# A three-layer decoder on one core: the last steps of its first stage in a hand-written order per engine

## The chip, the cores and the metric

The kernel runs on one core of a Trainium2 chip. The metric is the time of one execution in device microseconds (us). The core has five engines with an instruction queue each, taken in order: TensorE (PE in the rows; its weight loads are PEld), VectorE (DVE), ScalarE (ACT), GpSimd (POOL) and SyncE (SP), which here only starts transfers. The engines meet by semaphores, and products land in eight PSUM banks of 128 x 512 float32 words.

## The reference, cut to what matters

The input is x, 16 batches of 128 tokens with 256 features. It passes three layers, each followed by a layernorm of (input + layer).

```python
# layer 1, for each batch b
h        = layernorm(x) * g + b
lin_out  = linear_attention(h @ wq_lin, h @ wk_lin, h @ wv_lin)     # one division per token
win_out  = window_attention(h @ wq_loc, h @ wk_loc, h @ wv_loc)     # 16 heads
gate     = sigmoid(relu(concat(lin_out, win_out, h) @ wg1 + bg1) @ wg2 + bg2)
layer    = (gate * lin_out + (1 - gate) * win_out) @ wo + bo + x
x        = layernorm(x + layer)
# layer 2: cross-attention of x with a context, 16 heads
# layer 3: 32 experts, each token goes to 4 of them, plus a shared expert
```

To keep float32 accuracy most products are made of float16 halves: a value is cast to a "high" part, the difference to it is the "low" part, and a product is high x high + high x low + low x high.

## The kernel before, in words

There are three stages, one after the other: layer 1 (lines 180 to 1220), layer 2 with the routing (from line 1300 on), and the experts. Between the first and the second stands a barrier of all engines (lines 1233 to 1235, with the clearing of the semaphores between).

**The first stage as a pipeline.** One loop per engine runs over steps i; each step calls small functions for batches that lag behind i. A batch n is at normalisation in step n, at its scores in step n+3, has its attention weights transposed (`transposed`, L978) and applied (`weighted`, L990) in steps n+4 and n+5, has both branches transposed (`branches_T`, L1060) in step n+5 together with the first gate product (`gate1`, L1076), the second gate product (`gate2`, L1089) in step n+6, the output product (`out_proj`, L1100 and L1104) in step n+7, and its residual sum and statistics on VectorE (`yt_` L855, `st2` L862 and L865) in step n+8, followed on GpSimd by the reciprocal root (`pow2`, "vareps" and "rstd") and the normalisation (`x1`, L472). So batch 15, the last one, goes on until step 23, while there are fewer and fewer other batches to work on: this is the drain.

**What stands between the products of one batch.** `lwf` (L587) takes the transposed branches out of PSUM, `lwhi` (L593) casts them, `lwlo` (GpSimd, L428) takes the low part: then `gate1` may run. `z1f_` (L600), `z1hi` (L607) and `z1lo` (GpSimd, L451): then `gate2`. `gt_` (L616), then on GpSimd `ma`, `mb`, `mhi`, `mlo` (L398, L406, L480, L436), which blend the two branches: then `out_proj`. `ls` and `ld` (L414, L421) make sum and difference of the branches beforehand on GpSimd.

**What orders the work.** The order of the calls in each engine's loop, and the table `ORDERS`: it lists which products share a bank and in which turn. `Turns.wait` makes each wait until the one before it in the list has been read:

```python
["KV0", "WO", "Z2", "Z1"],      # one bank: out_proj, gate2 and gate1 take turns
```

**What the drain does besides.** In steps 20 to 22 the start of layer 2 for batch 0 (and parts for 1 and 2) is put between: on ScalarE eight casts of constants (L668 to L675), the casts of normalised input and context (`x1_high` L622, `c_high` L626); on VectorE their low parts (`x1_low` L869, `c_low` L873), `xq_low` (L877), `xk_low` (L883), the four minima (`x_mins`, L888) and their halves (L895, L897); on TensorE `x1_T` (L1115), `q_proj`, `k_proj`, `v_proj` (all L1124), the scores (L1163) and the transposed scores (L1185, L1188); on ScalarE `x1T_`, `xq_high`, `xk_high`, `xv_`, `minT_` and the exponentials `x_exps` (L657). `v_proj` for batches 0 and 1 is done here. The low halves of the second stage's weights come in 8 pieces, one per step on GpSimd (`low_part`, L367), the last two in steps 19 and 20.

**The second stage's start.** Its own loops (from L1415 on) skip what the drain has done: `FRONT = 2` batches of the projections, one of the scores. In step 4 TensorE does, in this order, the transposition of the minima (L1922), parts of the weighted sums (L1954), and the transposed scores (L1936).

## Time and profile before

| | us |
|---|---|
| median of 3 runs | 695.78 (695.25 to 698.1) |
| the profiled execution, its own time | 693.8 |
| its span, first to last instruction | 692.0 |
| the drain: from the first step with no new batch's scores left to the barrier | about 232 to 271 of the span |

In the rows of this document PE, PEld, DVE, ACT and POOL are the engines as named above. A row of the timeline has the start in us from the span's start, the duration in us, engine, line, operation, output<-inputs, how many instructions are merged in it, and in brackets how long the engine sat idle before it and what released it. Durations of instructions on one engine overlap by some hundredths of a us, so the distance between two starts is what an instruction costs in a row of them. A row of stretches has the length, then for each engine the busy time with the count of instructions, the granted TensorE clock as a share of 2.4 GHz, the share of time in which the DMA engines were busy, and GB/s.

### The profile page before, as it was taken

The numbers are of one execution on the slowest core, as the hardware profiler recorded it, in microseconds if no ns is written. First come the engines' busy times: TensorE is split into PE (matmuls) and PEld (weight loads), VectorE is DVE, ScalarE is ACT, GpSimd is POOL, SyncE is SP. The second block draws the span as 40 slices with busy tenths as digits, with TensorE's granted clock in tenths as the row PEclk, the third lists the DMA queues.
The fourth block names the chain that finished last, engine by engine and source line by source line (L and its number), as shares of the span: only waits on it lengthen the run. The fifth ranks groups of instructions, "written<-read, shape, count | busy, mean of one in ns | idle before, by whom it ended". The sixth has DMA issues, their size and how long they took to land.

```text
span 692.0 us, 24587 instructions
## 1 busy us (share of the span) xinstructions
PE 579.0 (84%) x8258; PEld 482.5 (70%) x8258; DVE 516.0 (75%) x2068; ACT 481.9 (70%) x1325; POOL 474.5 (69%) x621
## 2 busy tenths in 40 slices
PE   1899999999999966988888887766668999999393
PEld 1678889888888755766656566545658988888272
DVE  2898989898888645589999998755756776767273
ACT  3799999999899944777777777655146776676022
POOL 4667899999988975243768676453706776777583
PEclk9999999999999998999999999976999999999697
DMA  9420000000200001324465645323678566672493
GB/s 302 118 57 3 2 3 4 2 3 16 56 2 3 3 17 32 85 80 146 133 199 158 194 140 186 110 88 114 205 202 234 162 181 191 174 204 83 147 331 129
DMA packets 53642, 77.81 MB, mean 112 GB/s; under 512 B 8457, under 2 KB 42513, under 8 KB 52881
## 3 DMA queue, kind: packets, MB, share of 16 engines
q1 hardware_dynamic: 42768, 56.50, 27.8%
q0 software_dynamic: 7632, 16.87, 6.8%
q10 hardware_dynamic: 3120, 2.88, 1.2%
q8 instruction: 69, 1.13, 0.7%
q14 instruction: 53, 0.43, 0.2%
HBM read 48.62 MB, written 27.49 MB: 110 GB/s over the span
## 4 chain that ended last, share of the span: by engine, by line
PE 25%; DVE 19%; issue 8%; POOL 3%; ACT 3%; DMA 1%; DVEq 0%; ACTq 0%; POOLq 0%; SPq 0%
PE bank L2379 6%; PE bank L2408 4%; DVE mnx L1639 4%; PE bank L2397 3%; PE bank L2348 3%; PE bank L1864 2%; DVE we_lo L1679 2%; PE bank L2017 1%; DVE min_hl L1646 1%; PE bank L2389 1%; POOL ya L2198 1%; DVE min_hl L1648 1%; PE bank L1913 1%; DVE aT L1672 1%; ACT aT L1565 1%
## 5 line engine op out<-in xcount | busy, mean ns | idle before, releaser
L2190 POOL DMA_INDIRECT y_rows<-front,ix x95 | 93.8, 987 | 50.7 <-DVE ix L2294 24.8
L572 ACT ACTIVATE sc<-sc,mn 128x128 f32<-128x128 f32 x256 | 82.6, 417 | 2.2 <-DVE mn L811 2.2
L1488 POOL DMA_INDIRECT x_rows<-rows,slot_ix x64 | 65.1, 1017 | 16.3 <-issue 13.8
L2215 ACT ACTIVATE sc<-bank 128x512 f16<-128x512 f16 x95 | 56.3, 595 | 26.5 <-DVE eh_lo L2298 21.9
L811 DVE CUSTOM_DVE_ANT_0 sc<-bank,rel 128x128 f32<-128x128 f32 x256 | 57.6, 286 | 0.8 <-issue 0.5
L820 DVE TENSOR_TENSOR pT_lo<-bank,pT_hi 128x512 f16<-128x512 f32 x64 | 43.1, 675 | 5.2 <-ACT pT_hi L579 5.1
L2290 DVE COPY front<-bank 128x256 f32<-128x256 f32 x63 | 26.7, 424 | 22.9 <-PE bank L2408 22.5
L1019 PE MATMUL bank<-hT,w_hi 128*128 128x128 f16 x384 | 42.7, 225 | 1.2 <-POOL hT L382 1.0
L579 ACT ACTIVATE pT_hi<-bank 128x512 f16<-128x512 f32 x64 | 38.5, 604 | 4.4 <-PE bank L978 4.2
L978 PE MATMUL bank<-ident,sc 128*128 128x128 f32 x256 | 39.4, 276 | 1.1 <-DVE k_lo L801 1.1
L2379 PE MATMUL bank<-we_hi,sc 128*128 x252 | 37.8, 273 | 1.6 <-ACT sc L2215 1.3
L1639 DVE TENSOR_REDUCE mnx<-bank 128x4 f32<-128x512 f32 x60 | 37.2, 682 | 2.4 <-PE bank L1913 2.3
L2397 PE MATMUL bank<-ident,hT 128*128 128x128 f16 x380 | 36.6, 219 | 2.3 <-DMA hT<-x_rows 1.8
L1458 POOL TENSOR_TENSOR we_lo<-east,we_hi 128x256 f16<-128x256 f32 x48 | 31.2, 683 | 7.0 <-ACT we_hi L1521 6.8
L1466 POOL TENSOR_SCALAR xvar<-xmv 128x1 f32<-128x1 f32 x16 | 3.6, 226 | 46.5 <-DVE xmv L1703 46.5
L2237 ACT ACTIVATE sc<-bank,fshift,frstd 128x256 f32<-128x256 f32 x16 | 9.0, 564 | 34.8 <-DVE fshift L2337 25.5
L1864 PE MATMUL bank<-w_hi,front 128*128 128x256 f16 x120 | 23.7, 294 | 11.2 <-DVE front L1805 11.2
L1553 ACT ACTIVATE sc<-bank 128x512 f32<-128x512 f32 x60 | 30.9, 602 | 2.9 <-PE bank L1939 2.5
L1521 ACT ACTIVATE we_hi<-east 128x256 f16<-128x256 f32 (+1 forms) x80 | 31.2, 454 | 1.8 <-DMA east<-in_experts 1.7
L1002 PE MATMUL bank<-w_hi,hT 128*128 128x256 f16 (+1 forms) x128 | 31.8, 331 | 0.3 <-DVE vlin L763 0.3
L1019 PEld LDWEIGHTS bank<-hT,w_hi 128*128 128x128 f16 x384 | 29.4, 101 | 2.3 <-DVE w_lo L726 1.3
L2397 PEld LDWEIGHTS bank<-ident,hT 128*128 128x128 f16 x380 | 27.7, 98 | 3.3 <-issue 2.5
(333 smaller groups left out, 2338.5 us busy)
## 6 DMA issues: line engine op xcount, KB each, us to landing
east<-in_experts SPq DMA_DIRECT2D x32, 384.0 KB, 3.3
hT<-x_rows SPq DMA_DIRECT2D x95, 129.0 KB
rows<-xhl SPq DMA_DIRECT2D x16, 512.0 KB, 4.5
hT<-y_rows SPq DMA_DIRECT2D x16, 512.0 KB, 5.4
x_rows<-pad_block SPq DMA_DIRECT2D x32, 129.0 KB, 2.8
wst<-in_wcat SPq DMA_DIRECT2D x8, 256.0 KB, 6.5
front<-in_ctx_t SPq DMA_DIRECT2D x16, 128.0 KB, 3.0
out<-sc ACTq DMA_DIRECT2D x16, 128.0 KB, 4.9
```

Of the source, the lines that this page charges most:

```text
L572: done = act.activation(sc[:, g, j], sc[:, g, j], ACT.Exp, bias=mn[:, n % 2, g, j:j + 1], scale=-1.0)
L579: act.activation(pT_hi[:, g % 2], pT_bank[g][:].rearrange("p (h k) -> p h k", h=GH), ACT.Copy).then_inc(pThi_r[g], 1)
L811: dve.tensor_tensor_reduce(out=sc[:, g, j], in0=sc_bank[g][:, j * P:(j + 1) * P], in1=rel[:, g, j], scale=-1.0, scalar=-NEG, op0=ALU.add, ...
L820: dve.tensor_tensor(pT_lo[:, g % 2], pT_bank[g][:].rearrange("p (h k) -> p h k", h=GH), pT_hi[:, g % 2], ALU.subtract).then_inc(pT_rd[g], 1)
L978: last = pe.transpose(pT_bank[g][:, j * P:(j + 1) * P], sc[:, g, j], ident[:])
L1019: last = pe.matmul(room[u][:, m * P:(m + 1) * P], w[:, k, col + m * P:col + (m + 1) * P], hT[:, n, hp, k], start=t == 0 and not bias, stop ...
L1488: pool.indirect_dma_start(shared.x_rows, bass.IndirectOffsetOnAxis(ap=slot_ix[:, n, k:k + 1], axis=0), rows4[:, q, k], None).then_inc(shar ...
L1639: dve.tensor_reduce(mnx[:, n % 2, g], sc_bank[g][:].rearrange("p (h k) -> p h k", h=GH), AX_X, ALU.min).then_inc(xmn_r[g], 1)
L2190: pool.indirect_dma_start(c.y_rows, bass.IndirectOffsetOnAxis(ap=ix[:, n % IX], axis=0), yo[:, n % YO], None, bounds_check=NDEST - 1, oob_ ...
L2215: act.activation(gT[:, n % U], GT_BANK[n % len(GT_BANK)], ACT.Copy).then_inc(gt_r, 1)
L2379: done = pe.matmul(GU_BANK[n % len(GU_BANK)][:, 0:2 * EI].rearrange("p (m w) -> p m w", m=2), gT[:, n % U, x_, k], E[y_][k][:, :, bass.ds( ...
L2397: done = pe.transpose(GT_BANK[n % len(GT_BANK)][:, part, k], xg.bitcast(F16)[:, n % G, (part * KT + k) * P:(part * KT + k + 1) * P], c.ide ...
```

## The change

- Every engine's loop of the first stage now ends before the drain (TensorE after step 18, the others after step 19), and what is left is written out as a list of calls per engine, in an order of its own. On TensorE `gate1(14)` is split in two halves with `weighted(15, ...)` between.
- Six late products no longer take turns in the shared bank: `out_proj(13)` goes to bank 1, `gate2(14)` to bank 0, `out_proj(14)` to bank 5; `gate1(15)`, `gate2(15)` and `out_proj(15)` stay in bank 4 with waits of their own.
- The eight casts of constants, `x1_high` and `c_high` for batches 0 and 1, the low parts of the last two weight pieces, and batch 15's `lwlo`, `z1lo`, blend (`mixture`), and the normalisation of batches 14 and 15 (`normal`) are on VectorE in place of ScalarE and GpSimd.
- `v_proj(1)` and its `xv_(1)` move to step 4 of the second stage. `v_proj(0)` uses bank 7. `q_proj`, `k_proj` and `v_proj` wait for 4 of the 8 weight pieces, not for all.

The diff, cut to its core (12 columns of indentation are taken away):

```diff
-FRONT, FRONT_X, FRONT_C, FRONT_S = 2, 3, 3, 1
+FRONT, FRONT_X, FRONT_C, FRONT_S, FRONT_V = 2, 3, 3, 1, 1
+FRONT_PIECES = -(-(2 * D + D) // 228)
...
-POOL_PIECES = {3: (6,), 4: (7, 8), 5: (9, 10), **{k: (k - 2,) for k in range(13, 21)}}
+POOL_PIECES = {3: (6,), 4: (7, 8), 5: (9, 10), **{k: (k - 2,) for k in range(13, 19)}}
+LATE_PIECES = (17, 18)
...
+first_values = banks[7]
...
+drain_room = {("WO", NB - 3): (banks[1], (pv_rd, NB)),
+              ("Z2", NB - 2): (banks[0], (emptied["S3"], NB)),
+              ("Z1", NB - 1): (banks[4], (emptied["Z1"], 2 * (NB - 1))),
+              ("WO", NB - 2): (banks[5], (front_emptied["XT"], 2)),
+              ("Z2", NB - 1): (banks[4], (emptied["Z1"], 2 * NB)),
+              ("WO", NB - 1): (banks[4], (emptied["Z2"], 2 * NB))}
+
+def room_of(u, n):
+    return drain_room[u, n][0] if (u, n) in drain_room else room[u]
...
-        for i in range(NB + 8):
+        for i in range(NB + 4):
...
+        lwlo(NB - 2)
+        ma(NB - 3)
+        mb(NB - 3)
+        mhi(NB - 3)
+        mlo(NB - 3)
+        ls(NB - 2)
+        pow2(NB - 4)
+        z1lo(NB - 2)
+        x1(NB - 4)
+        ls(NB - 1)
+        ld(NB - 1)
+        pow2(NB - 3)
+        ma(NB - 2)
+        mb(NB - 2)
+        mhi(NB - 2)
+        mlo(NB - 2)
+        x1(NB - 3)
+        pow2(NB - 2)
+        pow2(NB - 1)
...
-        for i in range(NB + 7):
-            if i == NB + 4:
-                act.activation(ident16[:], ident[:], ACT.Copy).then_inc(id16_r, 1)
-                act.activation(identb[:], ident[:], ACT.Copy).then_inc(idb_r, 1)
-                act.wait_ge(rc_in, 64)
-                act.activation(tri16[:], tri[:], ACT.Copy).then_inc(idb_r, 1)
-                act.wait_ge(front_set, 4)
-                act.activation(ones16[:], ones[:], ACT.Copy).then_inc(idb_r, 1)
-                for k in range(GH):
-                    act.activation(pick_min[:, k], ones[:], ACT.Copy, scale=par[:, 2 + k:3 + k]).then_inc(idb_r, 1)
-                for n in range(FRONT):
-                    x1_high(n)
-                    c_high(n)
+        for i in range(NB + 4):
             z1f_(i - 6)
...
+        x1T_(0)
+        z1f_(NB - 2)
+        z1hi(NB - 2)
+        x1T_(1)
+        lwf(NB - 1)
+        lwhi(NB - 1)
+        xq_high(0)
+        xk_high(0)
+        gt_(NB - 2)
+        z1f_(NB - 1)
+        z1hi(NB - 1)
+        xv_(0)
+        gt_(NB - 1)
+        x1_high(2)
+        c_high_again(2)
+        xq_high(1)
+        minT_(0)
+        xk_high(1)
+        for g in range(NG):
+            x_exps(0, g)
+        x1T_(2)
...
+        def x1_high(n):
+            dve.wait_ge(x1_ready, n + 1)
+            dve.tensor_copy(x1[:, n, 0], xs[:, n]).then_inc(x1hi_r, 1)
...
+        def mixture(n):
+            s = n % 2
+            dve.wait_ge(emptied["Z2"], 2 * (n + 1))
+            dve.wait_ge(ldif_r, n + 1)
+            dve.wait_ge(mixa, n)
+            dve.tensor_tensor(gt[:, s], gt[:, s], ldif[:, s], ALU.mult).then_inc(mixa, 1)
+            dve.wait_ge(mixa, n + 1)
+            dve.wait_ge(lsum_r, n + 1)
+            dve.wait_ge(filled["WO"], n - 1)
+            dve.wait_ge(mixlo_r, n)
+            dve.tensor_tensor(mix_hi[:, s], gt[:, s], lsum[:, s], ALU.add).then_inc(mixhi_r, 1)
+            dve.tensor_tensor(mix[:, s], gt[:, s], lsum[:, s], ALU.add).then_inc(mixb, 1)
+            dve.wait_ge(mixhi_r, n + 1)
+            dve.wait_ge(mixb, n + 1)
+            dve.tensor_tensor(mix_lo[:, s], mix[:, s], mix_hi[:, s], ALU.subtract).then_inc(mixlo_r, 1)
...
+        dve.tensor_copy(ident16[:], ident[:]).then_inc(id16_r, 1)
+        x1_high(0)
+        x1_low(0)
+        yt_(NB - 4)
+        st2(NB - 4)
+        p_low(NB - 1, 2)
+        p_low(NB - 1, 3)
+        lw0(NB - 1)
+        rs(NB - 1)
+        lw1(NB - 1)
+        x1_high(1)
+        x1_low(1)
+        c_high(0)
+        c_low(0)
+        dve.tensor_copy(identb[:], ident[:]).then_inc(idb_r, 1)
+        dve.wait_ge(rc_in, 64)
+        dve.tensor_copy(tri16[:], tri[:]).then_inc(idb_r, 1)
+        dve.wait_ge(front_set, 4)
+        dve.tensor_copy(ones16[:], ones[:]).then_inc(idb_r, 1)
+        for k in range(GH):
+            dve.tensor_scalar(pick_min[:, k], ones[:], par[:, 2 + k:3 + k], None, ALU.mult).then_inc(idb_r, 1)
+        lwlo(NB - 1)
+        xq_low(0)
+        yt_(NB - 3)
+        xk_low(0)
+        st2(NB - 3)
+        c_high(1)
+        c_low(1)
+        for c in LATE_PIECES:
+            low_part(c)
+        z1lo(NB - 1)
+        for g in range(NG):
+            x_mins(0, g)
+        x_min_parts(0)
+        mixture(NB - 1)
+        yt_(NB - 2)
+        st2(NB - 2)
+        yt_(NB - 1)
+        st2(NB - 1)
+        normal(NB - 2)
+        xq_low(1)
+        normal(NB - 1)
+        x1_low(2)
+        xk_low(1)
+        c_low_again(2)
...
+            if n == FRONT:
+                pe.wait_ge(emptied["WO"], NB - 1)
...
+        def v_proj(n):
+            pe.wait_ge(front_emptied["XPK"], 2 * (n + 1))
+            pe.wait_ge(clo_r, n + 1)
+            pe.wait_ge(w_lo_late, N1 + FRONT_PIECES - NPROJ)
...
-            pe.wait_ge(emptied["S3"], NB)
-            pe.wait_ge(pv_rd, NB)
+            pe.wait_ge(emptied["Z2"], 2 * (NB - 1))
+            pe.wait_ge(emptied["WO"], NB - 2)
             pe.wait_ge(emptied["NUM"], NB)
...
+        weighted(NB - 2, 2)
+        transposed(NB - 1, 0)
+        weighted(NB - 2, 3)
+        transposed(NB - 1, 1)
+        kv(NB - 1)
+        branches_T(NB - 2)
+        out_proj(NB - 4)
+        weighted(NB - 1, 0)
+        gate2(NB - 3)
+        transposed(NB - 1, 2)
+        weighted(NB - 1, 1)
+        transposed(NB - 1, 3)
+        x1_T(0)
+        numerator(NB - 1)
+        gate1(NB - 2, (0,))
+        weighted(NB - 1, 2)
+        weighted(NB - 1, 3)
+        gate1(NB - 2, (1,))
+        branches_T(NB - 1)
+        x1_T(1)
+        q_proj(0)
+        out_proj(NB - 3)
+        k_proj(0)
+        gate2(NB - 2)
+        gate1(NB - 1)
+        x_scores(0)
+        v_proj(0)
+        gate2(NB - 1)
+        out_proj(NB - 2)
+        q_proj(1)
+        x_mins_T(0)
+        k_proj(1)
+        x_scores_T(0, (0, 1))
+        out_proj(NB - 1)
+        x_scores_T(0, (2, 3))
+        x1_T(2)
...
-            if i == NB + 5:
-                q_proj(0)
-                k_proj(0)
-                v_proj(1)
-                x1_T(1)
...
-            if i == NB + 6:
-                x_mins_T(0)
-                x1_T(2)
-                x_scores_T(0, (0, 1))
-                x_scores_T(0, (2, 3))
...
-            if i == NB + 4:
-                x1_T(0)
             gate1(i - 5)
-            if i == NB + 4:
-                v_proj(0)
-            if i == NB + 5:
-                x_scores(0)
-                q_proj(1)
-                k_proj(1)
             numerator(i - 4)
...
@@ xv_ on ScalarE and v_proj on TensorE, second stage @@
-        if FRONT <= n < NB:
+        if FRONT_V <= n < NB:
```

## Rows read from the trace of the kernel before

**Rows 1.** Stretches of 10 us: the steady loop and the middle of the drain.

```profile
210.00:220.00 10.00, 10.00 (x151) 8.53 (x150) 8.76 (x46) 9.79 (x29) 9.54 (x11) 1.00 0.02 5
...
250.00:260.00 10.00, 7.62 (x113) 6.83 (x114) 2.40 (x7) 4.81 (x14) 7.75 (x11) 0.99 0.01 2
```

**Rows 2.** Timeline of ScalarE and GpSimd: what ends the stage, what begins the next.

```profile
266.86 2.06 ACT L657 ACTIVATE sc<-bank 128x512 f32<-128x512 f32 x4 [0.40 <-PE bank L1188]
...
267.38 1.45 POOL L472 TENSOR_SCALAR xs<-yt,mv,rstd 128x256 f32<-128x256 f32 x1
270.68 0.11 POOL L1444 MEMSET gsum<- 128x16 f32 x1 [1.85 <-POOLq L1235]
```

**Rows 3.** Timeline of TensorE in the drain: the starts of late products and their waits.

```profile
244.50 0.18 PE L990 MATMUL bank<-vloc_hi,pT_hi 128*128 128x17 f16 x1 [1.63 <-DVE pT_lo L820]
...
246.59 0.94 PE L1060 MATMUL bank<-ident,lw 128*128 128x128 f32 x4 [1.03 <-DVE lw L834]
...
249.54 0.40 PE L1089 MATMUL bank<-z_hi,w_hi 128*128 128x128 f16 x2 [0.52 <-DVE yt L855]
...
251.38 0.40 PE L1076 MATMUL bank<-lwT_hi,w_hi 128*128 128x128 f16 x4 [0.49 <-ACT gt L616]
...
257.90 0.29 PE L1089 MATMUL bank<-z_hi,w_hi 128*128 128x128 f16 x2 [0.70 <-DVE yt L855]
...
263.45 0.42 PE L1100 MATMUL bank<-bo,share 128*128 128x256 f16 x1
```

**Rows 4.** Timeline of ScalarE and VectorE where the drain begins.

```profile
238.67 1.06 ACT L579 ACTIVATE pT_hi<-bank 128x512 f16<-128x512 f32 x2
...
240.42 1.27 ACT L675 ACTIVATE pick_min<-ones,par 128x128 bf16<-128x128 f32 x4
...
242.03 0.80 DVE L869 TENSOR_TENSOR front<-xs,front 128x256 f16<-128x256 f32 x1 [4.63 <-ACT front L622]
...
243.76 1.28 DVE L820 TENSOR_TENSOR pT_lo<-bank,pT_hi 128x512 f16<-128x512 f32 x2
```

**Rows 5.** VectorE's groups by shape over the whole run: busy us, mean ns.

```profile
L820 DVE TENSOR_TENSOR pT_lo<-bank,pT_hi 128x512 f16<-128x512 f32 x64 | 43.1, 675 | 5.2 <-ACT pT_hi L579 5.1
...
L888 DVE TENSOR_REDUCE mnx<-bank 128x4 f32<-128x512 f32 x4 | 2.5, 684 | 2.5 <-PE bank L1163 2.5
...
L735 DVE TENSOR_SCALAR bo<-rows 128x256 f16<-128x256 f32 x2 | 0.6, 284 | 0.0
```

**Rows 6.** Timeline of VectorE at the end of the drain.

```profile
265.21 0.41 DVE L855 SCALAR_TENSOR_TENSOR yt<-xs,bank 128x256 f32<-128x256 f32 x1
...
266.12 0.18 DVE L865 BATCH_NORM_AGGREGATE mv<-stats 128x2 f32<-128x6 f32 x1
...
266.53 0.87 DVE L883 SCALAR_TENSOR_TENSOR front<-bank,par,front 128x256 f16<-128x256 f32 x2
267.31 0.41 DVE L903 TENSOR_TENSOR front<-front 128x256 f16<-128x256 f32 x1
```

**Rows 7.** Timeline of GpSimd and VectorE where both read SBUF twice.

```profile
231.61 0.73 POOL L480 TENSOR_TENSOR mix_hi<-gt,lsum 128x256 f16<-128x256 f32 x1
232.42 1.00 POOL L436 TENSOR_TENSOR mix_lo<-mix,mix_hi 128x256 f16<-128x256 f32 x1
...
231.92 0.96 DVE L784 SCALAR_TENSOR_TENSOR kq<-kq,kq_exp 128x512 f32<-128x512 f32 x1
```

**Rows 8.** The line L784: all 16, duration in ns, least, median, most.

```profile
L784 DVE SCALAR_TENSOR_TENSOR kq<-kq,kq_exp x16: 681/895/1148, 29.3 to 231.9; 128x512 f32<-128x512 f32 x16
```

**Rows 9.** A stretch of 2 us in the drain, with the granted clock.

```profile
248.00:250.00 2.00, 1.48 (x10) 0.87 (x9) 0.88 (x3) 0.79 (x2) 1.76 (x3) 0.50 0.00 0
```

**Rows 10.** Timeline of TensorE: `v_proj(1)` begins, and what follows it.

```profile
255.40 0.38 PE L1124 MATMUL bank<-w_hi,front 128*128 128x256 f16 x2
...
256.06 0.39 PE L1115 MATMUL bank<-ident,front 128*128 128x128 f16 x4
```

**Rows 11.** The chain of waits in step 4 of the second stage.

```profile
277.36 0.27 PE bank L1936 x6
```

More of the change, by code:

```diff
@@ L910, in _ @@
                         st2(i - 8)
-                        if i == NB + 4:
-                            for n in range(FRONT):
-                                x1_low(n)
-                                c_low(n)
-                        if i == NB + 5:
-                            xq_low(0)
-                            xk_low(0)
-                        if i == NB + 6:
-                            for g in range(NG):
-                                x_mins(0, g)
-                            x_min_parts(0)
-                            x1_low(2)
-                        if i == NB + 7:
-                            xq_low(1)
-                            xk_low(1)
-                            c_low_again(2)
                         maxes(i - 4, 0)
@@ L1061, in branches_T, with turn, gate1 @@
                             last.then_inc(filled["TT"], 1)
-                    def gate1(n):
+                    def turn(u, n):
+                        if (u, n) in drain_room:
+                            pe.wait_ge(*drain_room[u, n][1])
+                        else:
+                            wait_turn(pe, u, n)
+                    def gate1(n, parts=range(KT)):
                         if live(n):
                             s = n % 2
-                            wait_turn(pe, "Z1", n)
+                            if 0 in parts:
+                                turn("Z1", n)
                             if n == 0:
@@ L1069, in gate1 @@
                             pe.wait_ge(lwlo_r, n + 1)
-                            for m in range(KT):
+                            for m in parts:
                                 t = 0
@@ L1077, in gate1 @@
                                         t += 1
-                            last.then_inc(filled["Z1"], 1)
+                            if KT - 1 in parts:
+                                last.then_inc(filled["Z1"], 1)
                     def gate2(n):
@@ L1119, in front_products @@
                     def front_products(u, lhs, rhs, tiles, width):
+                        bank = first_values if u == "XPV" else front_room[u]
                         for m in range(tiles):
@@ L1123, in front_products @@
                                 for k in range(KT):
-                                    last = pe.matmul(front_room[u][:, m * width:(m + 1) * width], lhs(x_, k, m), rhs(y_, k, m), start=t == 0, stop=t == 5)
+                                    last = pe.matmul(bank[:, m * width:(m + 1) * width], lhs(x_, k, m), rhs(y_, k, m), start=t == 0, stop=t == 5)
                                     t += 1
@@ L1190, in x_scores_T @@
                                         done.then_inc(front_filled[f"T{j}"], 1)
-                    for i in range(NB + 7):
+                    for i in range(NB + 3):
                         weighted(i - 5, 2)
```

77 lines of the change are left out of this document (37 added, 40 removed).

## The prediction

> **What bounds the kernel now.** I read the stretches of time first. In the steady loop of the first stage all four engines are 86 to 100% busy [rows 1]; in the drain VectorE works 2.40 us of 10, ScalarE 4.81, and TensorE has gaps. The kernel's time is there the latency of batch 15's chain through four engines, not any engine's work. Then the timeline at both sides of the barrier: ScalarE's last exponentials end at 268.92, GpSimd's last normalisation at 268.83, and the second stage begins at 270.68 [rows 2]. The barrier adds 1.8 us, and nothing of the second stage can start before it, so every us by which the last engine ends earlier is a us off the whole time, unless the second stage gets longer.
>
> Then TensorE's waits in the drain, in order of time [rows 3]: the weights of batch 15 at 244.50, held by VectorE's low part; the transposed branches at 246.59; `gate2(14)` at 249.54, which waits until VectorE has read another product in the same bank; `gate1(15)` at 251.38, behind ScalarE's reading of that bank; `gate2(15)` at 257.90, the bank again; `out_proj(15)` at 263.45. Their root is at the start [rows 4]: ScalarE has cast batch 15's last weights at 239.73 and then does casts of constants and of inputs, VectorE sits 4.63 us idle for the first of these, at 242.03, with `p_low(15, 2)` and `(15, 3)` queued behind, which start at 243.76 though the first of ScalarE's two casts was ready halfway, at 239.3.
>
> **The change, part by part.** I lay the new lists of calls out in time, each instruction at its duration in the rows, from where the engines stand at the same point of the old order (up to there nothing changes).
>
> *The head.* In VectorE's list nothing stands between it and `p_low(15, 2)` that waits for ScalarE: it starts at 239.3 in place of 243.76. From there to the transposed branches took 2.83 us [rows 3, 4]; I take 3.2, since the second pair of `weighted` now stands behind the first half of `gate1(14)` on TensorE (1.0 us, most of it beside VectorE's work). The branches are transposed at 242.5, 4.1 us earlier. The eight casts that left ScalarE free it to copy and cast the branches at 244.2 to 245.5.
>
> *VectorE becomes the queue that sets the end.* From 239.3 on its list is nearly full, so I add it up. A 128x512 instruction from PSUM costs 0.60 from start to start (0.675 less some 0.07 of overlap) [rows 5], a difference of 128x256 0.34, the pair of `xk_low` 0.78 (266.53 to 267.31), `yt` with both statistics 1.09 [rows 6]. A cast from SBUF to SBUF on VectorE is not in the trace. Its nearest row is the one-input form of the same shape, 0.284 [rows 5]: I take 0.22 from start to start, 0.15 for 128x128; the upper bound is the two-input form, 0.34 and 0.22. The list: low parts, divisions and branches of batch 15 3.2; x1 of batch 1 and context of batch 0 (two casts, two differences with a wait on each cast) 1.3; seven constants 1.1; `lwlo(15)` 0.6; `xq_low(0)`, `yt(13)`, `xk_low(0)`, statistics 2.0; context of batch 1, the two weight pieces, `z1lo(15)` 2.2; four minima (0.60 each) [rows 5] and their halves 2.9; the blend 1.6; `yt` and statistics of 14 and 15 2.2; the two normalisations, `xq_low(1)`, 0.5 of waiting for GpSimd's last root, `x1_low(2)`, `xk_low(1)`, `c_low_again(2)` 3.1. Sum 20.2.
>
> *The wait for the port.* One of VectorE's instructions with two inputs in SBUF starts at 231.92 while GpSimd's `mix_hi` runs until 232.34 [rows 7]; it takes 0.96, where the least of the 16 is 0.681 [rows 8]. GpSimd's next one, at 232.42, takes 1.00 in place of 0.7. So each waits for the other. The median of the 16 is 0.895, a wait of 0.2; the most is 0.47. In the new list some 22 instructions of VectorE read SBUF alone, 13 two-input ones of GpSimd lie in the same 20 us. Laid side by side, five of VectorE's meet one of GpSimd's (two constants, two weight pieces, `z1lo(15)`), for 0.1 to 0.5 each: 2.0 in all. Bounds: 0, and twice that.
> The Trainium skill ("SBUF — State Buffer", section "Who interferes with whom") says that the port pair is locked for a whole instruction and that a VectorE copy or cast, too, can take it. It speaks against putting these casts on VectorE; the rows above agree for two inputs (0.96 against 0.681), and no row shows it yet for a large cast.
>
> *Cover for the rest.* TensorE does the same products; by its list it waits for VectorE before `gate2(15)` (about 2 us), `out_proj(14)` (0.7) and the last `x1_T` (2.5), so the bank waits of rows 3 are gone and cost nothing. If VectorE were faster, TensorE's and ScalarE's own order would end within a us of it. GpSimd loses 1.1 us of weight piece before `lwlo(14)`, the two last pieces and most of batch 15; its list has gaps of over 3 us. SyncE's two context loads wait for `c_low(0)` and `c_low(1)`: these come at 243.9 and 249.1, 12 us before their data are needed at the barrier.
>
> *The clock.* In the drain TensorE was granted 1.2 GHz, half of its 2.4, from 248 to 250 [rows 9], after the gaps of 1.63 and 1.03 us at 244.50 and 246.59 with few products between [rows 3]. The new order leaves no such gap early, but one of 2 us before `gate2(15)`. I count 0.6 for a stretch at half clock, mostly behind VectorE's work; bounds 0 and 1.7.
>
> *Moved across the barrier.* `v_proj(1)` costs 0.66 (255.40 to 256.06) [rows 10]. In step 4 of the second stage it stands just ahead of the transposed scores, which are on the chain at 277.36 [rows 11]: +0.65. Bounds: 0 (if it falls into a wait) and 1.2 (with its read `xv_` in front of the exponentials).
>
> **The sum.** 239.3 + 20.2 + 2.0 + 0.6 = 262.1 in place of 268.9: -6.8. With +0.65 it is -6.2. On the profiled execution's 693.8 that is 687.6; the median of the runs is 2.0 above that execution (695.78), so 689.6 for the median. About 0.5%, 3.5 us, is what a measurement of this kernel can tell from no change.
>
> Ends: low with no port waits, no clock loss and a free `v_proj(1)`, 689.6 - 2.0 - 0.6 - 0.65 = 686.4; high with casts at their upper bound (+0.9), port waits doubled (+2.0) and the clock at its bound (+1.1), 693.6.
>
> **The rivals.**
> *The port eats it.* Each of the 13 two-input instructions of GpSimd holds VectorE up once, by its full 0.6: 7.8 in place of 2.0. For it: VectorE's list is back to back, so somebody is always waiting. Against it: the median wait of 0.2 in a loop in which GpSimd was 95% busy [rows 1, 8]. It gives 689.6 + 5.8 = 695.4, no change. Chance 0.12. By the Trainium skill's rule ("SBUF — State Buffer", the same section) whoever starts first holds the pair; no row shows which of two waiting engines gets it next.
> *The second stage gives back.* With `v_proj(1)` and `xv_(1)` put into step 4, the cast of context 3 is late and step 5 waits for it too. Against it: nothing else in step 4 waits for that cast. Price 0.66 + 0.4 + about 2: 692.5. Chance 0.10.
> *Slower: TensorE at half clock.* The new list has gaps of up to 2.5 us in which TensorE waits for VectorE. If one of these drops the clock for the rest of the drain, the products from 243 on, some 12 us of work, take twice as long (rows 9 show 1.2 GHz for a whole stretch); of the 12 us added, the gaps cover 5.4. It decides once more than half of that work runs low: +6.8 in the drain, and if the second stage's first 7 us of products start low as well, +3.7 more: 700.1. Against it: the old drain idled more and kept 2.4 GHz in the rest of the stretch 250 to 260, 0.99 [rows 1]. Chance 0.06.
>
> **How the numbers follow.** The forecast has 0.72. Nearly all of it, and half of the second rival, is over 3.5 us faster: 0.78. The port, the other half of the second rival and the forecast's upper tail are no change: 0.17. Slower 0.05. The range takes the ends of the forecast and the second rival: 686.4 to 693.5; outside are the port and the clock.
>
> **What would show it.** Right: `branches_T(15)` near 242.5, `gate1(15)` near 246.5, `gate2(15)` near 252, `out_proj(15)` near 256.5, the second stage's first instruction near 264; VectorE over 85% busy from 240 to 262; two-input rows on VectorE of up to 1.1 us for 0.7. Wrong: TensorE's waits on VectorE adding up to more than 7 us, GpSimd's rows of 0.7 grown to over 1 in general, a granted clock of 0.5 in more than two stretches of the drain, or the second stage longer than before by over 1.5 us.

## The result, and the profile after

| | before | after |
|---|---|---|
| median of 20 runs each, us | 697.02 (692.59 to 701.16) | 693.61 (686.56 to 695.34) |
| the profiled execution, its own time | 693.8 | 694.66 |
| its span | 692.0 | 692.9 |

The ratio is 0.9944, with a 95% interval of 0.9925 to 0.9963: a gain of 0.56%, some 3.9 us. (The ratio isn't the quotient of the two medians, which would give 3.4 us.) On the median of 695.78 that the prediction went by this is 691.9, against 689.6 forecast and inside the range of 686.4 to 693.5. Taken as it stands, the measured median of 693.61 is a tenth of a us above that range, since before's own median over 20 runs lies 1.2 us above that of the first three. The profiled execution shows no gain at all (694.66 against 693.8), though its drain is 7.4 us shorter: its second stage is longer. That is what the experiments had to explain.

To compare executions, whose starts lie up to 1.5 us apart, I count the drain from one instruction that no order touches: VectorE's `kq` of batch 15, at 231.92 before [rows 7] and 232.56 after (first row below). This is the timeline of the changed kernel by engine, VectorE first, then TensorE, ScalarE and GpSimd.

```profile
232.56 0.95 DVE L805 SCALAR_TENSOR_TENSOR kq<-kq,kq_exp 128x512 f32<-128x512 f32 x1
...
239.91 1.29 DVE L841 TENSOR_TENSOR pT_lo<-bank,pT_hi 128x512 f16<-128x512 f32 x2 [1.88 <-ACT pT_hi L611]
...
244.47 0.22 DVE L1015 CAST tri<-tri 128x128 f16<-128x128 f32 x1
244.60 0.70 DVE L1017 CAST ones<-ones 128x128 f16<-128x128 f32 x1
...
249.46 1.70 DVE L747 TENSOR_TENSOR w_lo<-wst,w_hi 128x456 f16<-128x456 f32 x2
251.09 0.94 DVE L940 TENSOR_TENSOR z_lo<-z1f,z_hi 128x256 f16<-128x256 f32 x1
...
255.43 0.42 DVE L952 TENSOR_TENSOR mix_hi<-gt,lsum 128x256 f16<-128x256 f32 x1
...
261.72 0.41 DVE L968 TENSOR_TENSOR front<-front 128x256 f16<-128x256 f32 x1
...
243.24 0.63 PE L1154 MATMUL bank<-ident,lw 128*128 128x128 f32 x4
...
247.06 0.38 PE L1177 MATMUL bank<-lwT_hi,w_hi 128*128 128x128 f16 x4
...
252.17 0.27 PE L1191 MATMUL bank<-z_hi,w_hi 128*128 128x128 f16 x2 [1.42 <-DVE z_lo L940]
...
257.13 0.28 PE L1202 MATMUL bank<-bo,share 128*128 128x256 f16 x1
...
261.16 0.38 PE L1219 MATMUL bank<-ident,front 128*128 128x128 f16 x4 [2.10 <-DVE front L890]
...
264.83 1.47 PE L2035 MATMUL bank<-front 32*128 32x256 f16 x24
...
261.59 0.60 ACT L660 ACTIVATE front<-bank 128x512 f16<-128x512 f16 x1 [1.40 <-PE bank L1219]
...
263.93 0.11 POOL L1566 MEMSET gsum<- 128x16 f32 x1 [3.70 <-POOLq L1357]
```

The second VectorE row answers to the last of [rows 4]; TensorE's rows are the transposed branches, `gate1(15)`, `gate2(15)`, `out_proj(15)` and the last `x1_T`, which answer to [rows 3]. None of them waits for a bank any more; what is left are waits for VectorE's results, of 1.42 us ahead of `gate2(15)` and of 2.10 ahead of the last `x1_T`, and one of 0.50 for GpSimd's `mlo` ahead of `out_proj(14)`. Counted from `kq`:

| us from `kq` | branches | `gate1(15)` | `gate2(15)` | `out_proj(15)` | second stage begins |
|---|---|---|---|---|---|
| before | 14.67 | 19.46 | 25.98 | 31.53 | 38.76 |
| forecast | 10.6 | 14.6 | 20.1 | 24.6 | 32.0 |
| after | 10.68 | 14.50 | 19.61 | 24.57 | 31.37 |

The drain came out as forecast, step by step, within 0.7 us. Now the stretches of the changed kernel: the drain, the barrier, and one in the second stage (the columns are those of [rows 1]).

```profile
240.00:262.00 22.00, 17.45 (x300) 14.86 (x298) 20.01 (x53) 11.75 (x30) 14.56 (x22) 0.99 0.05 15
262.00:264.00 2.00, 0.00 (x0) 0.00 (x0) 0.14 (x1) 0.18 (x1) 0.07 (x2) 0.50 0.00 0
...
304.00:306.00 2.00, 2.00 (x50) 1.91 (x48) 1.83 (x15) 1.12 (x3) 0.67 (x1) 0.50 0.01 3
```

VectorE is busy 20.01 of 22 us (8.60 in the kernel before over the same stretch, at a granted clock of 0.89) and the clock stays at 2.4 GHz, 0.99 granted. TensorE, idle at the barrier, is at 1.2 GHz (0.50) when the second stage starts, so that its first scores take 1.47 us (row at 264.83). That is no loss against before, whose second stage starts at half clock too:

```profile
271.57 1.47 PE L1913 MATMUL bank<-front 32*128 32x256 f16 x24
```

But a stretch from 302 to 312 runs at half clock too, in which one step of the second stage takes 14.7 us instead of 12.1. The clock line of the changed kernel's page shows where in the span this is (40 slices of 17.3 us):

```profile
PEclk9999999999999997979999999776999999999697
```

The 7s and the 6 in slices 16, 18 and 26 to 28 are the barrier, the stretch at 302, and 433 to 485 us, in which steps 14 and 15 of the second stage lie. Before's line has an 8 in slice 16, 7 and 6 in slices 27 and 28, and the same digits in the last three.

### The profile page after: what moved, and what is told of

The parts are those of the page before. It is cut to its first block, busy times and chain, and to the rows that moved or that the text cites. A ratio compares the mean times of both kernels' runs of the same rounds, so it can differ in the third digit from the quotient of the medians.

```text
span 692.9 us, 24589 instructions
## 1 busy us (share of the span) xinstructions
PE 583.7 (84%) x8258; PEld 484.3 (70%) x8258; DVE 525.3 (76%) x2090; ACT 479.1 (69%) x1313; POOL 465.6 (67%) x611
## 4 chain that ended last, share of the span: by engine, by line
PE 26%; DVE 17%; issue 9%; POOL 3%; ACT 3%; DMA 2%; SPq 1%; DVEq 0%; ACTq 0%; POOLq 0%
PE bank L2501 6%; PE bank L2530 4%; DVE mnx L1761 4%; PE bank L2519 3%; PE bank L2470 2%; PE bank L1986 2%; PE bank L2139 2%; DVE we_lo L1801 1%; PE bank L2058 1%; DVE min_hl L1768 1%; PE bank L2035 1%; POOL ya L2320 1%; PE bank L2511 1%; DMA hT<-x_rows 1%; DVE min_hl L1770 1%
## 5 line engine op out<-in xcount | busy, mean ns | idle before, releaser
L1986 PE MATMUL bank<-w_hi,front 128*128 128x256 f16 x124 | 26.0, 309 | 11.2 <-DVE front L1927 11.2
```

The costliest lines, as they stand in the source:

```text
L1986: last = pe.matmul(room[u][:, m * width:(m + 1) * width], lhs(x_, k, m), rhs(y_, k, m), start=first and t == 0, stop=t == 5)
```

## The experiments

One table for all. "Drain" is from `kq` to the second stage's first instruction; "first step" the distance between the first minima of the second stage's first two batches; "14+15" the two steps before the last of the second stage's statistics; "rest" from the second stage's first instruction to the end of the span. One profiled execution each, except the medians; the ratios are those of the measurement, with their 95% intervals, and again not quotients of medians.

| kernel | drain | first step | 14+15 | rest | that execution | median, ratio to before |
|---|---|---|---|---|---|---|
| before | 38.76 | 8.8 | 32.6 | 421.3 | 693.80 | |
| e9a, e9b, e9c: before again | 38.85, 40.08, 40.17 | 8.8, 8.8, 8.8 | 32.5, 32.7, 32.5 | 422.2, 422.0, 422.0 | 694.24, 696.58, 696.10 | |
| after | 31.37 | 9.7 | 36.1 | 429.0 | 694.66 | 693.61, 0.9944 |
| e1: after again | 31.39 | 9.5 | 35.4 | 427.1 | 692.40 | 692.36, 0.9948 [0.9925, 0.9971] |
| e2: `v_proj(1)` back in the drain | 31.60 | 8.4 | 36.7 | 427.4 | 693.04 | 691.58, 0.9913 [0.9879, 0.9947] |
| e3: weight pieces on GpSimd | 31.81 | 9.7 | 32.5 | 423.5 | 688.74 | 692.80, 0.9939 [0.9916, 0.9961] |
| e4: products as filler | 31.40 | 9.6 | 36.9 | 426.0 | 691.63 | 692.09, 0.9911 [0.9878, 0.9944] |
| e5: all in one bank | 32.30 | 9.7 | 32.5 | 423.7 | 690.56 | |
| e6: constants on ScalarE | 31.31 | 9.3 | 36.8 | 426.7 | 692.22 | |
| e7: before, casts on VectorE | 40.14 | 8.8 | 32.9 | 427.2 | 701.32 | |
| e8: e2 with filler | 31.51 | 11.1 | 36.1 | 430.5 | 695.82 | 689.82, 0.9896 [0.9865, 0.9927] |
| e10: e2 and pieces on GpSimd | 30.88 | 8.6 | 36.8 | 428.3 | 693.66 | 691.11, 0.9907 [0.9874, 0.9940] |

### Is the longer second stage chance? The changed kernel again (e1), and before three times (e9)

Edit of e1: none to the changed kernel.

> The changed kernel unaltered, a second profiled execution and a second set of times. Theory A (the drain gave what it was costed at, and the rest of the forecast was lost to TensorE's clock in the later stages, which differs from execution to execution): the second stage's first instruction is again near 264 us of the span (263.93 in the first execution, 270.68 before), and the steps of the second stage that run at the full clock are as long as before; the stretches at half clock lie elsewhere than at 302 to 312. Rival B (the change itself makes the later stages longer): the second stage is longer in the same step again, 14.7 us between the minima of steps 6 and 7 where before has 12.0.

The drain repeats to 0.02 us (31.39), and the second stage is long again, 427.1, though this time without a stretch at half clock between 300 and 320. What repeats is the first step (9.5 against 8.8) and steps 14 and 15 (35.4 against 32.6).

Edit of e9a, e9b and e9c: none to the kernel before.

> The kernel before, unaltered, profiled again for the length of its later stages (421.3 us from the second stage's first instruction to the end in the first profiled execution; 427 to 429 in two executions of the changed kernel). Theory A (the difference is TensorE's clock, which falls differently in each execution): this execution takes 421 to 428, and the steps 14 and 15 of the second stage are either 16 or 18 us long. Rival B (the change makes them longer): 421 to 422 again.

> As e9a_before, a third execution of the kernel before. Theory A: 421 to 428, not the same as e9a_before. Rival B: 421 to 422.

> As e9a_before, a fourth execution of the kernel before. Theory A: 421 to 428. Rival B: 421 to 422.

All four executions of the kernel before agree within 0.9 us from the second stage on (421.3 to 422.2), with 32.5 to 32.7 for steps 14 and 15. So e9's rival B held, and e1's length of 427.1 speaks for its rival B too, though at another step than 6 to 7. Before's drain varies more (38.8 to 40.2, mean 39.5), with TensorE's clock. These are the whole drains of the first execution and of e9b as stretches:

```profile
231.92:270.68 38.76, 27.53 (x400) 23.29 (x396) 17.66 (x46) 22.58 (x65) 29.88 (x42) 0.91 0.03 9
...
232.77:272.85 40.08, 29.07 (x400) 24.80 (x396) 17.53 (x46) 22.60 (x65) 29.88 (x42) 0.86 0.03 8
```

The two executions with 0.91 and 0.90 granted take 38.8 and 38.9 us, the two with 0.86 and 0.87 take 40.1 and 40.2. So against before's own spread the changed drain gains 8.1 us, not 7.4; and since it keeps 2.4 GHz from 240 to 261, some part of that gain is half clock that the old drain had and the new one has not. No run separates it. The longer second stage isn't chance of one profile: it belongs to the new kernels, in most of their executions.

How TensorE's clock makes the difference is seen best between e1 and e3, which do the same up to there. First e1, in stretches of 2 us around step 14:

```profile
426.00:428.00 2.00, 0.86 (x19) 0.42 (x17) 2.00 (x4) 1.01 (x3) 0.71 (x2) 1.00 0.01 4
428.00:430.00 2.00, 0.00 (x0) 0.00 (x0) 1.90 (x4) 0.00 (x0) 1.97 (x3) 0.97 0.18 66
430.00:432.00 2.00, 1.54 (x15) 0.95 (x15) 0.64 (x2) 1.07 (x3) 1.83 (x3) 0.50 0.17 15
...
434.00:436.00 2.00, 2.00 (x49) 1.71 (x45) 1.26 (x5) 0.98 (x3) 0.00 (x0) 0.50 0.86 310
...
440.00:442.00 2.00, 2.00 (x26) 1.81 (x25) 1.10 (x3) 0.56 (x1) 0.95 (x3) 0.97 0.53 175
```

The same stretches of e3:

```profile
426.00:428.00 2.00, 0.91 (x20) 0.47 (x17) 2.00 (x4) 1.06 (x3) 0.66 (x1) 1.00 0.01 4
428.00:430.00 2.00, 0.00 (x0) 0.00 (x0) 1.90 (x4) 0.00 (x0) 1.96 (x3) 1.00 0.18 66
430.00:432.00 2.00, 1.50 (x15) 0.95 (x15) 0.69 (x2) 1.03 (x3) 1.83 (x3) 0.57 0.03 5
...
434.00:436.00 2.00, 2.00 (x78) 1.80 (x70) 1.44 (x6) 1.63 (x5) 0.00 (x0) 1.00 0.87 309
```

And of e9b, one of the executions of before, where the same place lies some 8 us later:

```profile
440.00:442.00 2.00, 2.00 (x21) 1.10 (x20) 1.23 (x6) 1.97 (x4) 1.70 (x2) 0.50 0.66 160
442.00:444.00 2.00, 2.00 (x57) 1.38 (x57) 0.84 (x5) 1.32 (x4) 0.03 (x1) 0.78 1.06 388
```

In all three TensorE has just been idle (0.00 busy from 428 to 430 in the first two, from 436 to 438 in e9b), and then it is at 1.2 GHz. In e3 and e9b 2.4 GHz is back after some 3 to 4 us (1.00 from 434 on in e3, 0.78 from 442 to 444 in e9b); in e1 only after 10, and in the meantime a stretch of 2 us holds 49 matmul records where e3's holds 78. From 426 to 428 the busy times of e1 and e3 agree within 0.05 us in every column. So it isn't the work at this place that decides. Nor is it the chip: on each of the three chips on which the experiments ran there are profiled executions with short steps and with long ones. Of the 14 executions, all seven with 32.9 us or less for the two steps are before's, e3, e5 and e7; the other seven, 35.4 to 36.9, all have the new drain.

The last two columns of the table say which of them is typical. Before's four, at 693.8 to 696.6, with short steps, are the middle and the lower half of its runs. e3's profiled execution, with short steps, is the fastest of its 12 (median 692.80); those of after, e1, e2, e8 and e10, with long steps, lie at or above their kernels' medians, that of e4 half a us below. The mean granted clock of every execution says the same: of the 32 of the changed kernel (20, and e1's 12) the four under 690 us have 0.962 to 0.966 over the span, all others 0.959 or less; e3 and e5, with short steps, have 0.960 and 0.962, the new drain with long steps 0.947 to 0.957. So the new kernels mostly lose the 3 to 4 us, and sometimes do not. How often before loses them in executions that weren't profiled isn't shown; its median of 697.02 over 20 executions is above all four. What decides it stays open: the stage starts 7 to 8 us earlier, but e1 and e3 start it within 0.15 us of each other (263.5 and 263.4) and part all the same.

### What does `v_proj(1)` cost in the second stage? (e2)

```diff
-FRONT, FRONT_X, FRONT_C, FRONT_S, FRONT_V = 2, 3, 3, 1, 1
+FRONT, FRONT_X, FRONT_C, FRONT_S, FRONT_V = 2, 3, 3, 1, 2
...
         xv_(0)
+        xv_(1)
         gt_(NB - 1)
...
         v_proj(0)
+        v_proj(1)
         gate2(NB - 1)
```

(with the waits of `v_proj` and `q_proj` on each other's reads set to the new counts)

> v_proj(1) is done in the drain again, in TensorE's wait ahead of gate2(15). If v_proj(1) costs what its place in step 4 of the second stage says: the first step of the second stage (minima to minima) goes back from 9.7 us to about 8.8 us, the second stage begins no later than in the changed kernel (263.9), and the time is 0.65 us under the changed kernel's. If it was hidden in the second stage: the same step stays at 9.7 at an equal clock and the time does not move.

The first step falls from 9.7 and 9.5 to 8.4. In the drain `v_proj(1)` fills part of the wait for `z_lo`, and the drain is 0.2 longer because the last `x1_T` runs at half clock (0.58 us in place of 0.38). The chain of waits of the changed kernel shows it in step 4, between the transposed minima and the transposed scores:

```profile
270.14 0.36 PE bank L2076 x8
270.50 0.76 PE bank L1986 x6
271.26 0.36 PE bank L2076 x8
```

0.76 us of the chain is `v_proj(1)` itself; with what came around it, 1.1 to 1.3 of the step. It was put at 0.65, with 1.2 as the bound. In the whole time this doesn't show: 0.9913 and the change's 0.9944 have intervals that overlap.

### What is the port worth? Weight pieces on GpSimd together (e3), and apart at quiet places (e10)

"The port" is, as in the prediction, the way into SBUF for which VectorE and GpSimd wait on each other.

```diff
@@ GpSimd's list @@
         x1(NB - 3)
+        for c in LATE_PIECES:
+            low_part(c)
         pow2(NB - 2)
@@ VectorE's list @@
         c_low(1)
-        for c in LATE_PIECES:
-            low_part(c)
         z1lo(NB - 1)
```

> The low parts of the last two weight pieces go from VectorE's list (1.63 us ahead of z1lo(15)) to GpSimd's gap after its last normalisation. If VectorE's list sets the end from there on (my step): z1lo(15), gate2(15) and all behind them start 1.6 to 2.0 us earlier (the port wait of GpSimd goes too), and the second stage begins near 262.2. Rival: the chain TensorE to ScalarE to VectorE sets it, z1hi(15) ends at 250.34, and only 0.8 us are to be had.

`gate2(15)` is 1.1 us earlier (18.54 from `kq`), not 1.6 to 2.0: `z_lo` now waits 0.82 us for ScalarE's `z_hi`, as the rival had it. And the second stage is 0.4 later all the same. The timeline of e3, VectorE and then GpSimd:

```profile
249.38 0.58 DVE L942 TENSOR_TENSOR z_lo<-z1f,z_hi 128x256 f16<-128x256 f32 x1 [0.82 <-ACT z_hi L641]
...
253.36 1.16 DVE L954 TENSOR_TENSOR mix_hi<-gt,lsum 128x256 f16<-128x256 f32 x1
254.44 1.27 DVE L955 TENSOR_TENSOR mix<-gt,lsum 128x256 f32<-128x256 f32 x1
...
253.16 2.27 POOL L380 TENSOR_TENSOR w_lo<-wst,w_hi 128x456 f16<-128x456 f32 x2
```

GpSimd's two pieces, over 1 us each, now lie beside batch 15's blend, and the two additions take 1.16 and 1.27 where each takes 0.42 alone (row at 255.43 above): 1.6 us lost at the end, where nothing can take it up, for 1.1 gained before.

```diff
@@ e2, and in GpSimd's list @@
         ld(NB - 1)
+        low_part(LATE_PIECES[0])
         pow2(NB - 3)
...
         mlo(NB - 2)
+        low_part(LATE_PIECES[1])
         x1(NB - 3)
@@ v_proj(1) behind gate2(NB - 1), xv_(1) behind gt_(NB - 1); VectorE's list without low_part @@
```

> The two late weight pieces on GpSimd, but each where VectorE reads PSUM and not SBUF twice (one before the root of batch 13, one beside VectorE's minima), and v_proj(1) in the drain, in TensorE's wait behind gate2(15). If the port collision is what ate the gain when both pieces stood beside the blend: batch 15's kq to the second stage takes 29.7 to 30.0 us (31.4 in the changed kernel), the blend's instructions are back at 0.42 each, the second stage's first step is 8.4 to 8.8, and the time is about 0.989 of before. If not: 31.4 or more.

The pieces were to stand where VectorE reads PSUM. Of the 1.5 us that this should free, 0.5 came (30.88; the expectation had 29.7 to 30.0). The rest went into single instructions that met one of GpSimd's, not always a weight piece, as in e10's timeline of VectorE:

```profile
249.01 0.52 DVE L929 CAST front<-front 128x256 f16<-128x256 f32 x1
...
250.56 0.84 DVE L943 TENSOR_TENSOR z_lo<-z1f,z_hi 128x256 f16<-128x256 f32 x1 [0.56 <-ACT z_hi L641]
...
254.61 0.62 DVE L950 TENSOR_TENSOR gt<-gt,ldif 128x256 f32<-128x256 f32 x1
```

and into the wait for ScalarE's `z_hi` ahead of the second of these. The blend's two additions are back at 0.42. The time, 0.9907 of before, can't be told from e2's 0.9913.

### Can products without use keep the clock up? (e4, e8)

```diff
+        def filler(count):
+            for _ in range(count):
+                pe.matmul(banks[4][:, D:2 * D], ident16[:], w2_hi[:, 0, 0:D], start=True, stop=True)
...
+        pe.wait_ge(emptied["Z1"], 2 * NB)
+        filler(12)
         gate2(NB - 1)
...
         x_scores_T(0, (2, 3))
+        pe.wait_ge(emptied["WO"], NB)
+        filler(18)
         x1_T(2)
+        filler(6)
```

These 36 products land in a half of a bank that nobody reads; they only keep TensorE at work in its waits.

> 36 filler products without use (256 columns, into the unused half of a bank) in TensorE's waits ahead of gate2(15) and around x1_T(2); nothing waits for them. If the half clock at the start of the second stage (0.50 from 262 to 268 in the changed kernel) follows from the idle 2 us before the barrier: the first 3 us of the second stage run at 2.4 GHz, its first scores take 0.8 us and not 1.47, and the second stage is about 1.5 us shorter. Rival: the barrier's own gap of 2 to 3 us is enough for the drop, and nothing changes.

The second stage's first scores take 0.84 us in place of 1.47, and its first minima start 1.67 us after the stage's first instruction, not 2.39. The timeline of e4 has the scores as

```profile
264.54 0.84 PE L2044 MATMUL bank<-front 32*128 32x256 f16 x24
```

But its stretches of 2 us show that the half clock only comes later:

```profile
262.00:264.00 2.00, 0.07 (x1) 0.00 (x0) 0.00 (x1) 0.05 (x1) 0.19 (x4) 1.00 0.00 0
...
266.00:268.00 2.00, 2.00 (x24) 1.42 (x21) 1.96 (x4) 0.87 (x3) 0.37 (x1) 0.50 0.44 149
```

The first step stays at 9.6, so what is won is the 0.7 before it, half of what was expected. It has nothing to do with the change: before has the same 1.47.

e8 has e2's edits and this filler behind the last output product only, 17 and 7 products around `x1_T(2)`.

> The changed kernel with v_proj(1) in TensorE's wait ahead of gate2(15) and 24 filler products in its waits around x1_T(2). Alone the first took 1.1 us off the first step of the second stage and the second 0.7 us off the time to its first minima; together 1.8 us under the changed kernel, near 0.991 of before. If the half clock only moves to a later product: the gain of the second is given back and it is 0.9925.

In its profiled execution, the slowest of its six, the half clock met the transposed scores, which stand on the chain, and the first step took 11.1 us. A row of e8's timeline of TensorE:

```profile
270.31 0.50 PE L2068 MATMUL bank<-front 32*128 32x128 f16 x6
```

0.50 us for six of them, 0.33 at 2.4 GHz. Over its runs e8 is the fastest kernel of the study: 0.9896 of before, against 0.9944 for the change. The intervals of the two still overlap (0.9927 and 0.9925), and that of e8 overlaps e2's: it is shown that it beats before, and not shown that its filler adds to e2.

### What are the spare banks worth? (e5)

```diff
-            drain_room = {("WO", NB - 3): (banks[1], (pv_rd, NB)),
-                          ("Z2", NB - 2): (banks[0], (emptied["S3"], NB)),
...
-                          ("WO", NB - 2): (banks[5], (front_emptied["XT"], 2)),
+            drain_room = {("WO", NB - 3): (banks[4], (emptied["Z1"], 2 * (NB - 1))),
+                          ("Z2", NB - 2): (banks[4], (emptied["WO"], NB - 2)),
...
+                          ("WO", NB - 2): (banks[4], (emptied["Z2"], 2 * NB)),
```

All six late products share bank 4 again, each behind the reading of the one before; the order of all lists stays.

> The changed kernel with its six late products back in the one shared bank, each waiting for the read of the one before it; the written order stays. If the spare banks are what lets the order gain: gate2(14) waits for yt(13) behind lwlo(15) in VectorE's list, gate1(15) for gt(14), out_proj(14) for gt(15), and the second stage begins 3 us or more later than in the changed kernel, counted from batch 15's kq (31.4 us there, 38.8 before). If the order alone does it: 31.4 to 32.

The bank waits are back, in e5's timeline of TensorE:

```profile
247.92 0.29 PE L1191 MATMUL bank<-z_hi,w_hi 128*128 128x128 f16 x2 [1.24 <-DVE yt L876]
...
249.49 0.40 PE L1177 MATMUL bank<-lwT_hi,w_hi 128*128 128x128 f16 x4 [0.72 <-ACT gt L648]
...
253.38 0.27 PE L1191 MATMUL bank<-z_hi,w_hi 128*128 128x128 f16 x2 [0.19 <-DVE z_lo L940]
```

`gate1(15)` starts 2.1 us later (16.64 from `kq`), but the wait for `z_lo` ahead of `gate2(15)` shrinks from 1.42 to 0.19, and the second stage only starts 0.9 later (32.30), between the two forecasts and near that of the order alone. Of the 7.4 us, spare banks give 0.9, on top of the new order and the moved work.

### What do the casts do? Back on ScalarE (e6), and moved alone (e7)

e6 is the changed kernel with the seven casts of constants (all but `ident16`) behind ScalarE's `x1T_(0)`.

```diff
@@ ScalarE's list @@
         x1T_(0)
+        act.activation(identb[:], ident[:], ACT.Copy).then_inc(idb_r, 1)
...
+        for k in range(GH):
+            act.activation(pick_min[:, k], ones[:], ACT.Copy, scale=par[:, 2 + k:3 + k]).then_inc(idb_r, 1)
         z1f_(NB - 2)
@@ VectorE's list: the same casts taken away ahead of lwlo(NB - 1) @@
```

> Seven of the eight casts of constants go back to ScalarE, into its 2.6 us of waiting after x1T_(0). My reading of the new trace: lwlo(15) starts when ScalarE's lwT_hi is there (246.11), not when VectorE is free, so 1.9 us less of work ahead of it brings at most 0.2 us: kq to second stage 31.2 to 31.4. Rival (VectorE's list sets the end from 239 on, as forecast): about 1.5 us less. It would be 0.5 us more if ScalarE gets late for z1f(14).

VectorE has 1.9 us less to do (244.33 to 246.23 in the changed kernel) and the drain is the same, 31.31 for 31.37. VectorE's timeline in e6:

```profile
245.95 0.69 DVE L940 TENSOR_TENSOR lwT_lo<-lwTf,lwT_hi 128x512 f16<-128x512 f32 x1 [1.72 <-ACT lwT_hi L625]
...
250.82 0.94 DVE L947 TENSOR_TENSOR z_lo<-z1f,z_hi 128x256 f16<-128x256 f32 x1
```

`lwT_lo` waits 1.72 us for ScalarE: what ended last there was the chain of transposed branches, TensorE and ScalarE, with VectorE's constants in its shadow. From `lwT_lo` on the list goes on as before.

e7 is the kernel before with the casts alone moved: ScalarE's eight constants and the casts for batches 0 and 1 go to VectorE, at the place in its loop where the low parts stood, ahead of `p_low(15, 2)`.

```diff
@@ ScalarE's loop @@
-            if i == NB + 4:
-                act.activation(ident16[:], ident[:], ACT.Copy).then_inc(id16_r, 1)
...
-                for n in range(FRONT):
-                    x1_high(n)
-                    c_high(n)
@@ VectorE's loop @@
             if i == NB + 4:
+                dve.tensor_copy(ident16[:], ident[:]).then_inc(id16_r, 1)
...
                 for n in range(FRONT):
+                    dve.tensor_copy(x1[:, n, 0], xs[:, n]).then_inc(x1hi_r, 1)
+                    dve.tensor_copy(c_hi[:, n], cst[:, n]).then_inc(chi_r, 1)
                     x1_low(n)
                     c_low(n)
```

> The kernel before with one part of the change alone: the casts of constants, x1_high and c_high of batches 0 and 1 on VectorE, all in front of p_low(15, 2); order and banks as before. Batch 15's branches are transposed about 3 us earlier than before (14.7 us after kq there, 10.7 in the changed kernel). If the turns in the shared bank bound what follows, half of that or less arrives at the barrier: kq to second stage 36 to 37.5, before 38.8, changed 31.4.

It is worse than before. The branches come at 16.05 from `kq`, not 14.67, and the second stage at 40.14. That is 1.3 to 1.4 us later than in the executions of before with the same clock in the drain (0.91 here; 38.8 and 38.9 there); before's two at 0.86 and 0.87 are as late as this. e7's timeline, VectorE and then GpSimd:

```profile
237.79 1.09 DVE L903 CAST identb<-ident 128x128 bf16<-128x128 f32 x1
238.81 1.19 DVE L905 CAST tri<-tri 128x128 f16<-128x128 f32 x1
239.92 0.76 DVE L907 CAST ones<-ones 128x128 f16<-128x128 f32 x1
...
245.44 1.27 DVE L810 TENSOR_TENSOR pT_lo<-bank,pT_hi 128x512 f16<-128x512 f32 x2
...
237.75 1.05 POOL L367 TENSOR_TENSOR w_lo<-wst,w_hi 128x456 f16<-128x456 f32 x1
238.75 1.16 POOL L428 TENSOR_TENSOR lwT_lo<-lwTf,lwT_hi 128x512 f16<-128x512 f32 x1
239.87 0.73 POOL L398 TENSOR_TENSOR gt<-gt,ldif 128x256 f32<-128x256 f32 x1
```

Each of the three casts starts within 0.06 us of one of GpSimd's instructions and ends within 0.1 of it: 1.09, 1.19 and 0.76 us for what takes 0.22 alone. The list ahead of `pT_lo` takes 7.8 us (237.60 to 245.44). By the changed kernel's rows it would be 3.9: 0.15 for each of eight constants, and 1.32 for each batch's two casts and two differences. So the casts on VectorE are no gain in themselves, in the old order. (e7's longer rest, 427.2, lies behind the last statistics of the second stage, in the experts; I didn't follow it.) In the changed kernel only two casts stand ahead of the low parts of batch 15 and the rest behind, in the shadow that e6 shows; that it is this place that makes them harmless is argued, no run has the new order without the moved work.

## Why the prediction was right, and where its sum was off

**The drain.** Right in its mechanism and in its sum. VectorE's list began at 7.35 us from `kq` (forecast 239.3, which is 7.38) and ended at 29.57; the last engine, ScalarE, at 29.63, where the forecast had 30.2. The 0.6 between has the size of the clock's term: it was put at 0.6, and 0.99 was granted from 240 to 262. The list itself took 22.2 us, as its 20.2 and the 2.0 for the port. That it fits to a tenth is partly luck: 1.4 of it are four short waits (0.40, 0.23, 0.38, 0.42), of which the sum had one of 0.5, and the instructions and the port were some 0.9 cheaper than counted.

**The port.** Sized right, and it was the term most worth having. From the rows: 0.48 in the cast of `ones` (0.70, where that of `tri` just before took 0.22), 0.52 in `z_lo` (0.94 for 0.42), 0.2 in one of the four `pick_min` (0.50, the others 0.27), and 0.5 in one of the two weight pieces (1.16, the other 0.63): 1.7 of the 2.0, in four meetings where five were counted. The rival in which it eats the gain had all 13 of GpSimd's meet one of VectorE's and fell with that number. e3 and e7 show how near it was: two pieces put beside the blend cost 1.6 us, and the casts beside GpSimd's run of work take 3.9 us more than the changed kernel's rows give for them.
By the Trainium skill ("SBUF — State Buffer", section "Who interferes with whom"), a VectorE cast can take the shared pair too, for a whole instruction. No row of before showed it; e7's three casts of 0.76 to 1.19 us for 0.22 agree.

**"VectorE becomes the queue that sets the end", from 239.3 on.** Half right. e6 shows that up to `lwT_lo` at 246.23 it was the chain over TensorE and ScalarE, and the constants cost nothing there. From there to the end VectorE is busy but for short waits, and e3 shows that even there `z_lo` could start only 0.7 us earlier before ScalarE's `z_hi` holds it. In the changed kernel both meet there: ScalarE's `lwT_hi` ends at 246.11 and VectorE is free at 246.23, so the sum came out though its reason held for one half only.

**"The bank waits of rows 3 are gone and cost nothing."** Near: e5 puts them at 0.9 us when they return, since most of such a wait then comes off the next wait for VectorE. The rest of the 7.4 to 8.1 us is the order, the work moved to VectorE, and the half clock that the old drain had and the new one hasn't; the runs didn't separate these, but for the casts alone (e7), which lose some 1.3.

**`v_proj(1)` in the second stage, +0.65.** Mis-sized: 0.76 on the chain, 1.1 to 1.3 by e2, at or just over the upper bound.

**The second stage otherwise: nothing.** This is the step that failed. The sum took it for granted that work after the barrier only moves. It gave back about 4 us by the medians (8.1 gained in the drain, 3.4 to 3.9 in the whole), 5 to 7 in the two profiled executions of the changed kernel: 0.7 to 0.9 in the first step, 2.8 to 3.5 in steps 14 and 15, in one execution 3 at 302 to 312, in the other 1.7 behind the second stage's last statistics (222.1 us to the end, where before has 219.6 to 220.8). The rival "the second stage gives back" has the nearest number (692.5; measured 691.9 on the same base), but not by its mechanism: no step waited for a late cast of context (the two steps behind the first take 9.9 and 10.9 us, in before 9.5 to 9.9 and 10.9). The rival of the half clock named the resource and put it in the wrong stage: the drain kept 2.4 GHz, and steps 170 us further on lost it for longer than before. Its second part, 3.7 us for a second stage that starts low, counted as new what before has already (0.50 granted there from 272 to 274, and in e9a from 270 to 276). The prediction did say that a second stage longer by over 1.5 us would make it wrong in that point, and it was. The range held the time because it reached to that rival; this was partly luck.

**The arithmetic.** Small slips that decide nothing: the forecast's own upper end is 693.6 and the range stops at 693.5; 0.72 and half of 0.10 give at most 0.77 for faster, not 0.78; the rival of the half clock has 0.06 and then 0.05, and its 12 less 5.4 is 6.6, not 6.8.

## What to carry to other kernels

In a drain, write out one list per engine and keep the last batch's chain ahead of everything that only has to be done by the end; here the spare banks were worth 0.9 us of 7.4, and moving casts without the new order lost some 1.3. Before moving casts and differences from ScalarE to VectorE, lay them beside GpSimd's instructions: the same cast is 0.22 or 1.19 us. And a gain of a per cent that shifts a later stage has to be measured over many executions and looked for in the later stages too: their clock may be granted otherwise, though none of their code has changed.

## What the runs showed that was not expected

- The same idle gap of TensorE (428 to 430) was followed by 1.2 GHz for 4 us in one kernel and for 10 in another, though the work just before it was the same.
- Filler products kept 2.4 GHz over the barrier (1.00 granted from 262 to 264 in e4), and the half clock came some 3 us later in e4 and 8 in e8, there on products that count more.
- Three casts on VectorE that started just behind an instruction of GpSimd ended just behind it too: 1.09 beside 1.05 us, 1.19 beside 1.16, 0.76 beside 0.73 (e7).
- Taking 2 us out of an engine's list that is 91% busy moved the end by 0.06 us (e6).
